# Two-layer attention and routing kernel: where a batch's statistics and its expert choice stand in the order of work

## The chip, the cores and the metric

The kernel runs on one core of one Trainium2 chip. The metric is the device time of one launch in microseconds. The core has five engines with a queue each: TensorE (PE, with its weight loads as PEld), VectorE (DVE), ScalarE (ACT), GpSimd (POOL) and SyncE (SP, which issues most of the transfers). Each queue is worked off in order, and the engines wait for one another with counting semaphores.

## What is computed

Input x is 4 batches of 1024 tokens of 128 numbers. Two layers follow, each of the form x = x + s · silu(f), where s is an attention and f a feed-forward network, both of the normalised xn = layernorm(x). Cut to what matters here:

```
xn = layernorm(x)
s  = attention(xn)            # 16 heads of 64, rope with cos/sin(position * rope_freqs), bias by distance
g  = silu(moe(xn))            # second layernorm with weights nw, nb; top-1 gate over 8 experts
x  = x + s * g
xn = layernorm(x)
# second layer: a recurrence over the tokens of each batch, per head (16 heads of 8)
q, k, v = xn @ q_w.T, xn @ k_w.T, xn @ v_w.T
lam = clip(sigmoid(decay) * (1 + 0.2 * sigmoid(tanh(xn @ cs_w1.T + b1) @ cs_w2.T + b2)), 0, 0.9995)
state_t = state_(t-1) * lam_t + k_t * v_t;   y_t = q_t . state_t;   s = y @ o_w.T
# its feed-forward network: one of 8 low-rank additions is chosen for each token
logits = xn @ gate_W.T + gate_b;   top1 = argmax(logits)
f  = relu(xn @ wi.T + wi_b + lora[top1](xn)) @ wo.T + wo_b
x  = x + s * silu(f)
```

## The kernel before

The program has three blocks one after the other: `before_heads` (the front: normalisation, routing, experts, q/k/v with rope), `attend` (the scores of 16 heads, by far the longest) and `layer1` (the second layer, here the last stage). A block starts when the block ahead of it has ended.

**Front.** Tokens lie on the partitions: a batch is 8 tiles of 128 tokens. SP issues the four batches of x first; ACT issues four small transfers of the rope frequencies. On VectorE `turns_of_angle` (L522 to L527, three instructions over 128x1024) multiplies positions by frequencies and finds the number of full turns; it waits for the frequencies. `stats(b)` (L494 to L508) waits for batch b of x, takes mean and variance (8 bn_stats, 8 bn_aggr) and five small instructions, and releases `var_ready`. GpSimd's `power(b)` then makes the reciprocal roots and the shift, ScalarE's `normalise(b)` the normalised rows, TensorE transposes them in the order of `turns` (xn0, xn1, a0, xn2, a1, xn3, a2, a3), ScalarE copies each out. `affine(b)` on VectorE makes the second norm. V rows are made between the transposes: TensorE, ScalarE (`v_high`), GpSimd (`v_low`), a transfer out. `reduced_angle` finishes the angles (they share tiles with nothing that the statistics use), the routing follows once all logits are there, and then 64 units of rope. The order on VectorE is written out: L537 `turns_of_angle()`, L538 `stats(0)`, then stats 1 and 2, affine 0, stats 3, affine 1 to 3, `reduced_angle`.

**Last stage.** It has N = 32 steps, 8 (FE) for each of 4 batches. Step n of the recurrence is: TensorE `made_rows(n)` (four matmuls for batch 0, L1710; two for the others, L1713), VectorE `scan(n)` (a product L1488 and a scan L1492), GpSimd's product with q (L1589), TensorE `share(n)` (16 matmuls, L1766), which stands two steps later in TensorE's queue. Two buffers are in rotation: made_rows(n) waits for scan(n-2), scan(n) for the product n-2.

Everything else is a list of jobs, `steps_of_layer1` (L1288), placed into the steps. In step n TensorE does made_rows(n), then the jobs of step n, then share(n-2). Each job writes the next of two PSUM banks in turn, so a job waits until the job two places before it has been taken out by ScalarE or VectorE. VectorE takes out the jobs of step n behind scan(n). The jobs:

- `turn`, `c1`, `c2`, `k`, `q`, `v`: transposes, decay, keys, queries and values of a batch. Those of batch 0 up to `c2` stand in `first`, ahead of step 0. TensorE's c1 waits itself for the transposes to be copied out; `z` does not.
- `z`: 16 matmuls, the logits and the low-rank products of a batch. ScalarE copies them out. `GATE_AT` names for each batch the step in which VectorE does `best_gate` (L1454: adds the bias, subtracts the maximum); ScalarE's Exp comes a step later, VectorE's `route` (L1461: first index of the maximum, one-hot, masked rows z_masked) two steps later.
- the network's feed, in eight halves j of 512 tokens: `zt` j (transposes z_masked, waits for `route`; VectorE takes out a part of it at L1503), `hid` j,0 to 3 (L1748 and L1749; the first waits for that part of zt), `out` j (32 matmuls, L1754). They are spread from step FFN_FROM to step 31 by a cost (zt 1, hid 2, out 7): `at[FFN_FROM + done * span // total].append(job)` with `span = FE * B - FFN_FROM`. After each second out ScalarE does the Silu of that batch (`SILU_AT`), and GpSimd the last product and sum of it.

Before the change the first steps hold (the number is the batch, or the half for zt, hid and out): step 0 both halves of q0 and of turn1; step 1 z0 z1 c1 v; step 2 c1 k v; step 3 k c2; step 4 c2 zt0 hid0,0 hid0,1; step 5 q hid0,2 hid0,3 zt1; step 6 q out0; step 7 hid1,0. In GATE_AT stand steps 1, 4, 12 and 20.

Between the loops VectorE has `stats(2)` in step 2 and `split_lora` (two small instructions) in step 1. ScalarE does norm(1) (8 instructions) ahead of its jobs of step 0.

Of the kernel before, what the change touches and what calls it, by code (L numbers as in the profile page):

```python
# [21 lines left out]
B, S, D = 4, 1024, 128  # L22
# [17 lines left out]
M_FIRST, W_SLOTS, E_SLOTS = 4, 10, 40  # L40
V_FIRST, V_MID = 18, 8
DMA = 16
FE, FFN_FROM = 8, 4
MAGIC = 12582912.0
TWO_PI_1 = 6.28125
TWO_PI_2 = 0.00193500518798828125
# [130 lines left out]
def before_heads(nc, K, io, sb, ps, sem):  # L177
# [116 lines left out]
    with nc.Block() as block:  # L294
# [196 lines left out]
        def _(v):  # L491
# [30 lines left out]
            def turns_of_angle():  # L522
                v.wait_ge(pos_made, 1)
                v.wait_ge(fr_in, 4 * DMA)
                ch.link(v.tensor_scalar(ang, pos, freq[:, 0:1], None, ALU.mult))
                ch.link(v.tensor_scalar(tn, ang, 1.0 / (2.0 * math.pi), MAGIC, ALU.mult, ALU.add))
                ch.link(v.tensor_scalar(tn, tn, MAGIC, None, ALU.subtract))  # L527

            def reduced_angle():
                for part in (TWO_PI_1, TWO_PI_2, TWO_PI_3):  # L530
# [3 lines left out]
                v.scalar_tensor_tensor(out=tn, in0=ang, scalar=-1.0, in1=ang, op0=ALU.mult,  # L534
                                       op1=ALU.max).then_inc(sin_arg, 1)

            turns_of_angle()  # L537
            stats(0)  # L538
            stats(1)
            stats(2)  # L540
            affine(0)
# [749 lines left out]
def steps_of_layer1():  # L1291

    at = [[] for _ in range(FE * B)]
    at[0] += [("q", 0, 0), ("q", 0, 1)]
    at[1] += [("z", 0, 0)]
    for b in range(1, B):
        n = FE * (b - 1)
        for f, jobs in enumerate(([("turn", b, 0), ("turn", b, 1)], [("z", b, 0), ("c1", b, 0)], [("c1", b, 1), ("k", b, 0)],
                                  [("k", b, 1), ("c2", b, 0)], [("c2", b, 1)], [("q", b, 0)], [("q", b, 1)])):
            at[n + f] += jobs  # L1300
    for b in range(1, B):
        for c in range(2):
            at[FE * (b - 1) + 1 + c].append(("v", b, c))
    feed = [("zt", 0, 0)] + [("hid", 0, i) for i in range(FT)]
    for j in range(NR):
        if j + 1 < NR:
            feed.append(("zt", j + 1, 0))
        feed.append(("out", j, 0))
        if j + 1 < NR:
            feed += [("hid", j + 1, i) for i in range(FT)]  # L1310
    cost = {"zt": 1, "hid": 2, "out": 7}
    total, done, span = sum(cost[job[0]] for job in feed), 0, FE * B - FFN_FROM
    for job in feed:
        at[FFN_FROM + done * span // total].append(job)
        done += cost[job[0]]
    return [("turn", 0, 0), ("turn", 0, 1), ("c1", 0, 0), ("c1", 0, 1), ("k", 0, 0), ("k", 0, 1), ("c2", 0, 0), ("c2", 0, 1)], at


def layer1(nc, K, io, sb, ps, sem):
# [7 lines left out]
    aux_made, by_act, by_dve, lam_raw = sem("aux_made"), sem("aux_by_act"), sem("aux_by_dve"), sem("lam_raw")  # L1327
# [39 lines left out]
    dve_takes = [job for job in jobs if job[0] in ("v", "zt", "out")]  # L1367
    act_nth = {job: k + 1 for k, job in enumerate(act_takes)}
    dve_nth = {job: k + 1 for k, job in enumerate(dve_takes)}
    GATE_AT = [1] + [FE * (b - 1) + 4 for b in range(1, B)]  # L1370
    SILU_AT = [step_of["out", 2 * b + 1, 0] + 1 for b in range(B)]

    def bank(job):
# [15 lines left out]
    with nc.Block() as block:  # L1389
# [48 lines left out]
        def _(v):  # L1438
# [72 lines left out]
            for n in range(N):  # L1511
# [3 lines left out]
                if n % FE == 2 and n // FE + 2 < B:  # L1515
                    stats(n // FE + 2)
                if n in GATE_AT:
                    best_gate(GATE_AT.index(n))
                if n - 2 in GATE_AT:
                    route(GATE_AT.index(n - 2))  # L1520
                if n == 1:
# [81 lines left out]
        def _(act):  # L1603
# [72 lines left out]
            for n in range(N):  # L1676
# [6 lines left out]
                if n % FE == 1 and n >= FE:  # L1683
                    take_share(n // FE - 1)
                if n - 1 in GATE_AT:
                    act.wait_ge(max_sub, GATE_AT.index(n - 1) + 1)
# [9 lines left out]
        @block.tensor  # L1696
        def _(pe):
            def made_rows(n):

                b, f = n // FE, n % FE  # L1700
                if n >= 2:
                    pe.wait_ge(scanned, n - 1)
                if n == FE:
                    pe.wait_ge(sel_made, 8)
                if n >= FE:
                    pe.wait_ge(vp_in[b % 2], vp_due(b))
                at = slice(64 * (f % 2), 64 * (f % 2) + 3 * H)
                for c in range(2):
                    if n < FE:
                        mm = pe.matmul(pj[n % 2][:, half(c)], wv[:, f, :], tokens(b, c),  # L1710
                                       start=True, stop=True)
                    else:
                        mm = pe.matmul(pj[n % 2][:, half(c)], SEL[at, :, :].rearrange("r h e -> r (h e)"),  # L1713
                                       VP[b % 2][at, f // 2, half(c)], start=True, stop=True)
                mm.then_inc(made, 1)

            def aux(job):
                kind, b, c = job
                a, dst = place[job], bank(job)
                if a >= 2:  # L1720
                    before = jobs[a - 2]
                    if before in dve_nth:
                        pe.wait_ge(by_dve, dve_nth[before])
                    else:
                        pe.wait_ge(by_act, act_nth[before])
                if kind == "turn":
                    pe.wait_ge(xn_ready, 2 * b + c + 1)
                    for k in range(4):
                        mm = pe.transpose(dst[:, k * P:k * P + P], XN[:, b % 2 * BT + 4 * c + k, :], K.ident[:])  # L1729
                elif kind == "c1":  # L1730
                    pe.wait_ge(by_act, act_nth["turn", b, c])
                    mm = pe.matmul(dst[0:D // 4, :], c1w[:], tokens(b, c), start=True, stop=True)  # L1732
                elif kind == "c2":
                    pe.wait_ge(by_act, act_nth["c1", b, c])
                    mm = pe.matmul(dst[:], c2w[:], C1[:, half(c)], start=True, stop=True)
                elif kind == "z":
                    for t in range(BT):
                        mm = pe.matmul(dst[:, t * NZ:t * NZ + NZ], XNT[:, (b * BT + t) * P:(b * BT + t + 1) * P], wz[:],  # L1738
                                       start=True, stop=True)
                elif kind == "v":  # L1740
                    mm = pe.matmul(dst[:], wvc[:].rearrange("p f h -> p (f h)"), tokens(b, c), start=True, stop=True)  # L1741
                elif kind == "zt":
                    pe.wait_ge(zm_ready, b // 2 + 1)
                    for t in range(4):
                        mm = pe.transpose(dst[0:3 * ER, t * P:t * P + P], ZM[:, 4 * (b % 4) + t, :], K.ident[:])
                elif kind == "hid":
                    pe.wait_ge(by_dve, dve_nth["zt", b, 0])
                    pe.matmul(dst[:], wi[:, c * P:c * P + P], XNT[:, half(b)], start=True, stop=False)  # L1748
                    mm = pe.matmul(dst[:], lb[:, c * P:c * P + P], ZT[:, half(b)], start=False, stop=True)  # L1749
                elif kind == "out":  # L1750
                    for i in range(FT):
                        pe.wait_ge(by_act, act_nth["hid", b, i])
                        for t in range(4):
                            mm = pe.matmul(dst[:, t * P:t * P + P], hT[b % 2][:, i, t * P:t * P + P], wo1[:, i, :],  # L1754
                                           start=(i == 0 and t == 0), stop=(i == FT - 1), skip_group_check=True)
                else:
                    mm = pe.matmul(dst[:], (wk if kind == "k" else wq)[:], tokens(b, c), start=True, stop=True)  # L1757
                mm.then_inc(aux_made, 1)

            def share(n):  # L1760
                b, f = n // FE, n % FE
                pe.wait_ge(weighed, n + 1)
                if f == 0 and b >= 1:
                    pe.wait_ge(s1_out, b)
                for t in range(BT):
                    mm = pe.matmul(so[:, t, :], WT[:, n % 2, t * P:t * P + P], wo[:, f, :],  # L1766
                                   start=(f == 0 and t % 4 == 0), stop=(f == FE - 1), skip_group_check=True)
                mm.then_inc(shared, 1)

            pe.wait_ge(w_in, 7 * DMA)  # L1770
            for job in first:
                aux(job)
            pe.wait_ge(vo_in, 2 * DMA)
            pe.wait_ge(wz_in, 2 * DMA)
            for n in range(N):
                made_rows(n)
                if n == 0:
                    pe.wait_ge(base_ready, 3)
                if n == FFN_FROM:
                    pe.wait_ge(lb_ready, 1)  # L1780
                for job in steps[n]:
                    aux(job)
                if n >= 2:
                    share(n - 2)
            share(N - 2)
            share(N - 1)
# [110 lines left out]
```

## Time and profile before

| | us |
|---|---|
| three runs | 1762.02, 1763.08, 1769.20 |
| median | 1763.08 |
| the profiled execution, its own time | 1762.21 |
| its span | 1760.5 |
| TensorE, VectorE, GpSimd, ScalarE busy | 1621.9, 1496.0, 1413.8, 1177.6 |

The profiled execution stands 1.7 us above its span and 0.9 us below the median. All times in the rows further down are microseconds from the start of the span. The page shows the span in slices: up to about 51 us is the front's normalisation, the rope units end at some 390 us, `attend` ends at 1515 us, the last stage takes the rest. A row of the timeline gives start, duration (of one instruction, or of a group that follows itself), engine, line, operation, tiles and shapes, and in brackets how long the engine was idle before it and what ended that.

### The profile page before, as it was taken

The numbers are of one execution on the slowest core, as the hardware profiler recorded it, in microseconds if no ns is written. First come the engines' busy times: TensorE is split into PE (matmuls) and PEld (weight loads), VectorE is DVE, ScalarE is ACT, GpSimd is POOL, SyncE is SP. The second block draws the span as 40 slices with busy tenths as digits, with TensorE's granted clock in tenths as the row PEclk, the third lists the DMA queues.
The fourth block names the chain that finished last, engine by engine and source line by source line (L and its number), as shares of the span: only waits on it lengthen the run. The fifth ranks groups of instructions, "written<-read, shape, count | busy, mean of one in ns | idle before, by whom it ended". The sixth has DMA issues, their size and how long they took to land. (4 is left out here: it accounts for less than half of the span.)

```text
span 1760.5 us, 39216 instructions
## 1 busy us (share of the span) xinstructions
PE 1621.9 (92%) x12064; PEld 890.5 (51%) x12064; DVE 1496.0 (85%) x3046; ACT 1177.6 (67%) x1806; POOL 1413.8 (80%) x820
## 2 busy tenths in 40 slices
PE   4879989858999999999999999999999999689998
PEld 3435655423555555555555555555555555346666
DVE  7778978996888989898898989888898989567876
ACT  6536544537877878777877877787787877644441
POOL 5676847857999999999999999999999999553554
PEclk9899999988999999999999999999999999889999
DMA  5466856768989889889889989989989988500110
GB/s 161 136 182 191 225 157 184 197 201 189 177 193 218 186 180 233 181 184 228 181 190 213 194 176 221 194 183 210 198 189 199 210 179 171 120 18 1 31 31 25
DMA packets 735171, 296.46 MB, mean 168 GB/s; under 512 B 630192, under 2 KB 697778, under 8 KB 735104
## 3 DMA queue, kind: packets, MB, share of 16 engines
q1 hardware_dynamic: 732304, 292.17, 73.9%
q0 software_dynamic: 2048, 3.15, 0.9%
q8 instruction: 24, 0.39, 0.1%
q10 hardware_dynamic: 768, 0.53, 0.1%
q14 instruction: 27, 0.22, 0.0%
HBM read 101.34 MB, written 58.85 MB: 91 GB/s over the span
## 5 line engine op out<-in xcount | busy, mean ns | idle before, releaser
L1271 POOL TENSOR_TENSOR probs_lo<-probs 128x1024 bf16<-128x1024 f32 x512 | 953.7, 1895 | 80.5 <-ACT probs L1235 79.9
L1235 ACT ACTIVATE probs<-scores,neg_max 128x1024 f32<-128x1024 f32 x512 | 588.2, 1149 | 220.1 <-DVE neg_max L1153 211.4
L1153 DVE CUSTOM_DVE_ANT_0 scores<-score_ps,bias_tab 128x1024 f32<-128x1024 f32 x512 | 620.3, 1220 | 76.9 <-issue 69.8
L1067 PE MATMUL score_ps<-x 128*128 128x512 bf16 x1024 | 308.5, 383 | 31.5 <-PEq L294 17.8
L1083 PEld LDWEIGHTS turn_ps<-ident_bf,probs 128*128 128x128 bf16 x4096 | 261.1, 98 | 146.0 <-issue 55.9
L1083 PE MATMUL turn_ps<-ident_bf,probs 128*128 128x128 bf16 x4096 | 313.9, 219 | 0.2
L1102 PE MATMUL pv_ps<-probs_t_hi,v_hi_lo 128*128 128x512 bf16 x1024 | 263.6, 380 | 0.3 <-DVE share L1185 0.3
L1242 ACT COPY probs_t_hi<-turn_ps 128x1024 bf16<-128x1024 bf16 x256 | 253.8, 991 | 0.0
L439 POOL TENSOR_TENSOR qk_parts<-rotated,qk_parts 128x1024 bf16<-128x1024 f32 x64 | 137.4, 2152 | 84.0 <-ACT qk_parts L872 83.6
L1168 DVE COPY probs_t_hi<-turn_ps 128x1024 bf16<-128x1024 bf16 x256 | 172.6, 674 | 0.8 <-PE turn_ps L1083 0.8
L1589 POOL TENSOR_TENSOR q_state<-state,q_t 128x1024 f32<-128x1024 f32 x32 | 76.0, 2375 | 107.2 <-PE s_ps L1766 71.3
L1075 PE MATMUL score_ps<-x 64*128 64x512 bf16 x1024 | 155.9, 383 | 0.0
L1102 PEld LDWEIGHTS pv_ps<-probs_t_hi,v_hi_lo 128*128 128x128 bf16 x1024 | 84.4, 98 | 115.0 <-issue 27.5
L1107 PE MATMUL pv_ps<-probs_t_lo,v_hi_lo 128*64 128x512 bf16 x1024 | 134.7, 385 | 0.0
L1067 PEld LDWEIGHTS score_ps<-x 128*128 128x128 bf16 x1024 | 74.9, 98 | 116.2 <-issue 45.5
L728 PE MATMUL turn_or_qk_ps<-xn_t,wqk 128*128 128x512 f32 x256 | 124.4, 611 | 7.5 <-DVE rotated L609 7.5
L1235 ACT ACTIVATION_READ_ACCUMULATOR probs<-scores,neg_max 128x1 f32 x512 | 96.2, 188 | 0.0
L1119 PE MATMUL pv_ps<-wo_parts,out_t_hi 128*128 (+1 forms) x512 | 90.9, 220 | 5.0 <-DVE out_t_lo L1176 2.3
L603 DVE TENSOR_TENSOR rope_cos<-turn_or_qk_ps,cos_table 128x1024 f32<-128x1024 f32 x64 | 78.0, 1219 | 17.5 <-PE turn_or_qk_ps L728 17.0
L609 DVE TENSOR_TENSOR rotated<-turn_or_qk_ps,rope_cos 128x1024 f32<-128x1024 f32 x64 | 78.4, 1225 | 15.3 <-POOL qk_parts L439 9.4
L1120 PE MATMUL pv_ps<-wo_parts,out_t_hi 128*128 (+1 forms) x512 | 89.3, 220 | 0.0
L1121 PE MATMUL pv_ps<-wo_parts,out_t_lo 128*128 (+1 forms) x512 | 89.1, 219 | 0.0
(236 smaller groups left out, 2311.1 us busy)
## 6 DMA issues: line engine op xcount, KB each, us to landing
x<-qk_parts SPq DMA_DIRECT2D x192, 256.0 KB, 3.4
qk_parts<-qk_parts SPq DMA_DIRECT2D x252, 128.0 KB, 2.5
v_hi_lo<-v_parts SPq DMA_DIRECT2D x64, 256.0 KB, 3.0
bias_tab<-bias_by_distance SPq DMA_DIRECT2D x64, 240.0 KB, 3.8
v_parts<-bias_tab SPq DMA_DIRECT2D x52, 256.0 KB, 2.9
probs_t_lo<-probs_lo SPq DMA_TRANSPOSE x512, 3.2
v_stacked<-v_three SPq DMA_DIRECT2D x72, 32.0 KB, 1.9
g<-in_x SPq DMA_DIRECT2D x4, 512.0 KB, 6.3
```

The source lines that it names most:

```text
L439: g.tensor_tensor(parts[n % QR][:, 2 - 2 * hi:4 - 2 * hi, :], rq[n % QR][:], parts[n % QR][:, 2 * hi:2 * hi + 2, :], ALU.subtract).then_in ...
L728: mm = pe.matmul(pp[n % 2][:, a * CH:a * CH + CH], K.wqk[:, g4, 2 * w + a, :], rows, start=True, stop=True)
L1067: pe.matmul(sp_[n % 2][:, cs], QB[s][:, q], KK[s][:, cs], start=True, stop=False)
L1075: mm = pe.matmul(sp_[i][:, cs], (QK, QB)[c][s][rows, q], (KK, QK)[c][s][rows, cs], start=False, stop=True)
L1083: mm = pe.transpose(tp[n % 2][:, k, :], PRB[n % NP][:, k * P:k * P + P], ident16[:])
L1102: mm = pe.matmul(ov[i][:], VV[h][:, k, :], PT[:, r:r + 4, k, :], start=(k == 0), stop=False, skip_group_check=True)
L1107: mm = pe.matmul(ov[c][c * DH:c * DH + DH], VV[h][:, k, 0:DH], LO[:, r:r + 4, k, :], start=False, stop=(k == BT - 1), skip_group_check=True)
L1153: v.tensor_tensor_reduce(SB[n % 2][:], sp_[n % 2][:], TB[s][:, j:j + S], -SCALE, 3.0e38, ALU.add, ALU.min, neg_max[:, n % 16:n % 16 + 1]). ...
L1168: v.tensor_copy(PT[:, n % U, :, :], tp[n % 2][:]).then_inc(hi_dve, 1)
L1235: act.activation(PR[n % NP][:], SB[n % 2][:], ACT.Exp, bias=neg_max[:, m:m + 1], scale=-1.0, accum_out=row_sum[:, m:m + 1]).then_inc(exped, 1)
L1242: act.copy(PT[:, n % U, :, :], tp[n % 2][:]).then_inc(hi_act, 1)
L1271: g.tensor_tensor(LQ[n % NL][:], PR[n % NP][:], PRB[n % NP], ALU.subtract).then_inc(low_made, 1)
```

## The change

It has four parts. In the front `stats(0)` stands ahead of `turns_of_angle()`. In the last stage the job z of batch 0 moves from step 1 to the head of step 0, with a wait of TensorE for the copy of that batch's second transposed half. `GATE_AT` for batch 0 moves from 1 to 0, and with it best_gate to step 0, Exp to step 1 and route to step 2. FFN_FROM goes from 4 to 5: the feed is spread over 27 steps instead of 28.

```diff
-FE, FFN_FROM = 8, 4
+FE, FFN_FROM = 8, 5
...
+            stats(0)
             turns_of_angle()
-            stats(0)
             stats(1)
             stats(2)
             affine(0)
...
     at = [[] for _ in range(FE * B)]
-    at[0] += [("q", 0, 0), ("q", 0, 1)]
-    at[1] += [("z", 0, 0)]
+    at[0] += [("z", 0, 0), ("q", 0, 0), ("q", 0, 1)]
...
-    GATE_AT = [1] + [FE * (b - 1) + 4 for b in range(1, B)]
+    GATE_AT = [0] + [FE * (b - 1) + 4 for b in range(1, B)]
...
                 elif kind == "z":
+                    pe.wait_ge(by_act, act_nth["turn", b, 1])
                     for t in range(BT):
```

After it the first steps hold: step 0 z0, both halves of q0 and of turn1; step 1 z1 c1 v; steps 2 and 3 as before; step 4 c2; step 5 q zt0 hid0,0 hid0,1; step 6 q hid0,2 hid0,3 zt1; step 7 out0. Of the later steps, 10 gets zt2 and out1 (they stood in 9), 17 gets zt4 and out3 (they stood in 16); from step 23 on only zt7 moves (from 26 to 27). Silu of the first batch goes from step 10 to 11, of the second from 17 to 18; the last two stay.

## Rows read from the trace of the kernel before

**Rows 1.** Busy time by engine in two stretches: from:to, length, busy (count), PEclk, DMA, GB/s.

```profile
70.00:400.00 330.00, 278.43 (x1021) 153.71 (x1022) 284.37 (x286) 153.20 (x222) 224.15 (x138) 0.95 0.68 188
...
1568.90:1747.00 178.10, 170.06 (x981) 115.92 (x981) 128.71 (x133) 71.20 (x109) 89.06 (x41) 0.99 0.09 22
```

**Rows 2.** Timeline of VectorE in the front.

```profile
7.54 0.75 DVE L525 TENSOR_SCALAR rotated<-rotated,freq 128x1024 f32<-128x1024 f32 x1 [7.54 <-DMA freq<-in_freqs]
...
9.79 1.65 DVE L498 BATCH_NORM_STATS2 ln_six<-g 128x6 f32<-128x128 f32 x8
...
12.94 1.64 DVE L498 BATCH_NORM_STATS2 ln_six<-g 128x6 f32<-128x128 f32 x8
...
19.65 2.19 DVE L517 SCALAR_TENSOR_TENSOR s<-g,ln_rstd,attn_nw_rows 128x128 f32<-128x128 f32 x8 [0.34 <-ACT g L810]
...
51.72 0.49 DVE L549 COPY logits<-step_ps 128x320 f32<-128x320 f32 x1 [4.52 <-PE step_ps L679]
```

**Rows 3.** Timeline of SP's queue: the four batches of x are issued.

```profile
0.82 3.81 SPq L308 DMA_DIRECT2D g<-in_x  x4
```

**Rows 4.** Issue to landing: the four transfers of x; the last of the frequencies.

```profile
DMA to landing us min/median/max: 4.0/6.3/7.9
...
freq<-in_freqs ACTq DMA_DIRECT2D x1, 0.1 KB, 5.2
```

**Rows 5.** Timeline of ScalarE in the front: the first two batches normalised.

```profile
16.34 6.33 ACT L810 ACTIVATE g<-g,ln_shift,ln_rstd 128x128 f32<-128x128 f32 x16 [12.35 <-POOL ln_shift L417]
```

**Rows 6.** Chain of work that ended last, early last stage: start, length, what.

```profile
1575.43 1.72 PE made_ps L1710 x4
1577.15 0.86 PE aux_ps L1757 x2
...
1580.61 1.79 PE s_ps L1766 x16
```

**Rows 7.** Timeline of TensorE, steps 0 to 4 of the last stage.

```profile
1537.16 1.14 PE L1729 MATMUL aux_ps<-ident,xn 128*128 128x128 f32 x8 [1.57 <-ACT q_t L1640]
...
1539.86 3.66 PE L1738 MATMUL aux_ps<-gate_lora_a,xn_t 128*128 128x40 f32 x32
...
1564.71 1.06 PE L1745 MATMUL aux_ps<-ident,z_masked 128*96 128x128 f32 x4 [4.39 <-DVE z_masked L1474]
1568.89 2.04 PE L1748 MATMUL aux_ps<-xn_t,wi 128*128 128x512 f32 x2 [3.12 <-DVE z_t_parts L1503]
```

**Rows 8.** Timeline of VectorE, steps 1 to 4, and step 6 for comparison.

```profile
1546.81 0.40 DVE L1457 TENSOR_TENSOR z_rows<-z_rows,gate_b 128x64 f32<-128x64 f32 x1
...
1547.65 0.41 DVE L1478 CAST lora_b_parts<-lora_b_f 96x512 bf16<-96x512 f32 x1
...
1548.81 1.23 DVE L1488 TENSOR_TENSOR made_ps<-made_ps,k_t 128x1024 f32<-128x1024 f32 x1
1550.07 2.29 DVE L1492 TENSOR_TENSOR_SCAN state<-lam,made_ps 128x1024 f32<-128x1024 f32 x1
...
1559.71 2.38 DVE L1466 TENSOR_TENSOR route<-route,iota 128x64 f32<-128x64 f32 x1
...
1589.40 0.23 DVE L1466 TENSOR_TENSOR route<-route,iota 128x64 f32<-128x64 f32 x1
```

**Rows 9.** Timeline of GpSimd: its product of step 3.

```profile
1559.67 2.34 POOL L1589 TENSOR_TENSOR q_state<-state,q_t 128x1024 f32<-128x1024 f32 x1 [3.77 <-DVE state L1492]
```

**Rows 10.** Timeline of ScalarE: norm(1), and the load ahead of Exp.

```profile
1533.46 3.18 ACT L1614 ACTIVATE xn<-x,ln_shift,ln_rstd 128x128 f32<-128x128 f32 x8
...
1553.61 1.28 ACT L1688 ACT_TABLE_LOAD   x1
```

**Rows 11.** Two stretches of 2 us in the last stage, columns as above.

```profile
1562.00:1564.00 2.00, 0.00 (x0) 0.00 (x0) 1.90 (x7) 0.00 (x0) 2.00 (x3) 0.86 0.00 0
1572.00:1574.00 2.00, 2.00 (x8) 1.19 (x7) 0.00 (x0) 0.55 (x2) 0.00 (x0) 0.58 0.25 52
```

**Rows 12.** TensorE's waits from 1570 to 1748: total us, times, longest.

```profile
PE aux_ps L1748 <- ACT lam L1636: 3.1, 3, 1.5
```

## The prediction

> **What bounds the kernel now.** I read the stretches first [rows 1]. In the front's 64 rope units (70 to 400 us) VectorE is busy 284 of 330 us, and in the last stage, from 1568.9 to 1747, TensorE 170 of 178. So the last stage is TensorE's from 1568.9 on; ahead of that the timelines show it waiting. Three places matter to the change.
>
> In the front VectorE's first instruction waits 7.54 us for the rope frequencies, and only behind the three angle instructions, at 9.79, does it begin on the first batch of x [rows 2]. That batch was issued at 0.82 and is the shortest of four landings, 4.0 us: it lay there from 4.8 [rows 3, 4]. ScalarE's normalising starts at 16.34, after 12.35 us of idleness put down to GpSimd's shift, the next link behind the statistics [rows 5]. VectorE then works through with 0.34 us of idleness before affine(0) at 19.65.
>
> In the last stage TensorE idles 4.39 us for the masked rows of route(0) and 3.12 us more for VectorE's part of zt0, which stands behind scan(4); hid0,0 starts at 1568.89 [rows 7]. VectorE is the bound of that stretch: its chain runs from scan(2) at 1548.81 without a gap through a v part, stats(2), scan(3), route(0), scan(4) and the zt part [rows 8].
>
> The clock: from 1562 to 1564 TensorE did nothing and its granted clock averaged 0.86, from 1572 to 1574 it was 0.58, though busy throughout [rows 11]. It had fallen from 2.4 to 1.2 GHz in the wait, and the first of hid0,0 took 2.04 us instead of about 1.
>
> **The change part by part.**
>
> *Statistics first.* Nothing is removed or added; stats(0) and the angles change places. stats(0) takes 12.94 - 9.79 = 3.15 us, the angles 9.79 - 7.54 = 2.25 [rows 2]. New order: stats(0) from about 4.95 to 8.1; the angles to 10.35 (the last frequencies, issued at some 2.2, take 5.2 and are there at 7.4 [rows 4], so they no longer hold anything up); stats(1) to 13.5 and stats(2) to 16.65. The last x, issued before 4.63, needs at most 7.9, so no batch is late. affine(0) wants the first normalised rows: GpSimd and ScalarE had them 16.34 - 9.79 = 6.55 us after stats(0) began plus half of the 6.33 us of two batches, now 4.95 + 6.55 + 3.2 = 14.7. So VectorE is the later, and affine(0) starts at 16.65 instead of 19.65: 3.0 earlier. Batch 1's statistics end at 13.5 instead of 9.79 + 2 x 3.15 = 16.1, only 2.6 earlier, but stats(3) and all that VectorE orders behind affine(0) comes 3.0 earlier. What then leads to the logits at 51.72 is a chain of transposes, copies, v parts and their transfers, each started by the one before. VectorE waits 4.52 us there for TensorE [rows 2], so the angles could end later, unseen. The logits come 3.0 earlier, less whatever the parts that move by 2.6 hold back. I take 2.95; the bounds are 1.5 (the clock, or a transfer of v that meets the early loads) and 3.2. Nothing behind it is tied to a fixed time, so rope units and scores pass it on.
>
> *Logits and routing a step sooner.* z0 costs half of 3.66 us for z0 and z1 = 1.8 [rows 7], now in step 0. Its new wait, for the copy of turn 0,1, is free: that copy is before step 0. But q0's second half now uses the bank that z0 leaves, and ScalarE copies z0 out only behind norm(1), 1533.46 + 3.18 = 1536.64 [rows 10], plus an estimated 0.45. The second q starts at about 1537.1, where the transposes started before, and these follow 1.1 later, as the two copies alternate. made_rows(1) is 1.1 late, step 1 is 1.8 shorter, so what follows in step 1 is 0.7 earlier. best_gate(0) leaves VectorE's step 1, where it takes 1547.65 - 1546.81 = 0.85 [rows 8], for the wait ahead of scan(1): free. Scan(2) starts 0.7 + 0.85 = 1.5 earlier, at 1547.3. Exp's table load of 1.28 [rows 10] now stands ahead of step 2's tanh, whose bank the second v part wants; I estimate 0.65 of VectorE's waiting from it (half of the load; the rest lies beside scan(2)). If tanh needs a load again, it is 1.28 more.
>
> route(0) stood against GpSimd's product: L1466 took 2.38 us and ended 0.1 after that product (1559.67 + 2.34 = 1562.01), where the same form takes 0.23 alone [rows 8, 9]. In step 2, behind stats(2), the product of that step is done by then, so I take 2.15 off; the bounds are 0 and 2.75.
>
> *The network a step later.* zt0's part on VectorE now stands behind scan(5), not scan(4). That is one more product and scan, 1550.07 - 1548.81 + 2.29 = 3.55 [rows 8], and best_gate(1) of step 4, about what best_gate(0) takes, 0.85; I take 0.75, since its first row already holds some waiting. hid0,0 starts at 1568.89 - 1.5 + 0.65 + 3.55 + 0.75 - 2.15 = 1570.2 (without the front's gain), **1.3 later** than now. But by then TensorE has done what it now does behind it: share(2) 1.79, made_rows(5) 1.72 and a q of 0.86 = 4.37 [rows 6]. Net 4.37 - 1.3 = **3.1 earlier**. The idleness moves: TensorE has no more work after zt0, about as long after made_rows(5) as now after made_rows(4), and I estimate one wait of 4 to 5 us, so its clock falls again, and the slow first two hid stay at their price.
>
> From there TensorE's work is the same in sum, in 27 steps instead of 28. It lost 178.10 - 170.06 = 8.0 us there [rows 1], the largest part 3.1 in three waits for the sigmoid copies [rows 12]. zt2 and out1 now share step 10 with a v part, zt4 and out3 step 17: each waits about 1 us for VectorE's part of v behind the scan. In return Silu leaves the steps of the c1 jobs. I take no change, with 2 us to either side. The tail from step 24 is as before.
>
> A rule is to be weighed here. That row of 2.38 beside 0.23, ending with the product, is a stall of a whole instruction. The Trainium skill, "SBUF — State Buffer", section "SBUF: two separate sides", says that a VectorE operation with two SBUF inputs and a GpSimd operation that reads SBUF exclude each other for a whole instruction. By that rule best_gate(0), right behind scan(0) when the product of step 0 starts, waits up to 2.3 us, and scan(1) begins at 1541.5 instead of 1541.2; the sum would be the same, since the v part behind it comes later anyway.
>
> **Sum:** 2.95 + 3.1 = 6.0; 1762.21 - 6.0 = 1756.2 for an execution like the profiled one, which is 0.9 under the median. I say **1756.5**.
>
> **The rivals.**
>
> *A, the clock holds.* If TensorE's wait for zt0 is short enough, hid0,0 and 0,1 run at 2.4 GHz and save about 2.4 more (the first alone 1.0 of 2.04 [rows 7]): 1753.8 or, with a better step pattern, 1752. Against it: I expect one wait of over 4 us, and 4.39 took the clock down. 0.13.
>
> *B, only the front gains.* The fuller steps 10 and 17 leave TensorE waiting 3 us more and eat the 3.1: 1759.3. For it: the bank order couples every job to VectorE's scan. Against: TensorE idles only 8.0 in 178 now. 0.19.
>
> *C, only the last stage gains.* The change doesn't do in the front what it says: the logits are bound by the v parts and their transfers, which wait for something other than VectorE. 1759.1. Against: ScalarE's first work waits on the statistics. 0.08.
>
> *D, slower.* Place: VectorE between scan(1) and zt0's part. best_gate(0), split_lora, stats(2) and route(0) all move against GpSimd's products, and each stalls a full 2.34 [rows 9]: 9.4 us. It decides from the point where hid0,0 starts 4.37 + 2.95 = 7.3 later than 1568.89. With all four it starts 1.3 + 9.4 = 10.7 later, the stage loses 9.4 - 3.1 = 6.3, the sum is 3.3 slower: 1765.5. Against: one such stall is seen there in five steps. 0.05.
>
> **Chances.** Forecast 0.55, own range 1754 to 1759; A 0.13, B 0.19, C 0.08, D 0.05. Low end: A with 2 us fewer waits, 1751.5. High end: B or C with the worse front and a run 0.9 above the profile, 1761.5. A measurement of this kernel can tell about 0.5% (8.8 us) from no change. Faster by more than that (under 1754.3) takes most of A and the forecast's lower edge: 0.17. Slower by more (over 1771.9) takes D with further loss: 0.03. Within: 0.80.
>
> **What would show it.** Right: bn_stats of the first batch at 4.9 to 5.0, angles from 8.1, affine(0) near 16.7, the logits' copy near 48.8; in the last stage (less the front's 3) best_gate(0) ahead of scan(1), TensorE's one wait of 4 to 5 us ahead of hid0,0, half clock behind it, made_rows(8) two to three us earlier than now. Wrong: the logits not 2.5 earlier; hid0,0 more than 4.4 later; TensorE's waits behind it well over 8 us; or a granted clock that stays full.

## The result, and the profile after

| | before | after |
|---|---|---|
| runs | 22 | 22 |
| median, us | 1767.27 | 1760.17 |
| lowest, us | 1762.02 | 1756.61 |
| the profiled execution, its own time | 1762.21 | 1762.45 |
| its span | 1760.5 | 1760.7 |

The ratio of the new kernel to the old one is 0.9968, with a 95% interval from 0.9956 to 0.998: 0.32% faster, less than the 0.5% that the prediction took as its bound. The interval lies below 1 all the same. The ratios are of fast runs alone: two slow ones of the kernel before, of 2690.35 us here and of 5571.03 beside runs 9 to 12 below, don't count in them. The means without them lie 5.6 us apart, the medians 7.1. The median of 1760.17 lies 1.2 above the range of 1754 to 1759 that the prediction gave. Yet the two profiled executions last the same, so a reader who had only these would find no gain. Why becomes clear from the trace, stretch by stretch.

**The front** did what the prediction says. Timeline of VectorE in the front, after (columns as in [rows 2]):

```profile
4.98 1.65 DVE L498 BATCH_NORM_STATS2 ln_six<-g 128x6 f32<-128x128 f32 x8 [4.98 <-DMA g<-in_x]
...
8.15 0.75 DVE L525 TENSOR_SCALAR rotated<-rotated,freq 128x1024 f32<-128x1024 f32 x1
...
16.70 2.19 DVE L517 SCALAR_TENSOR_TENSOR s<-g,ln_rstd,attn_nw_rows 128x128 f32<-128x128 f32 x8
...
48.67 0.49 DVE L549 COPY logits<-step_ps 128x320 f32<-128x320 f32 x1 [4.43 <-PE step_ps L679]
```

The first statistics start at 4.98 (forecast 4.95) and no longer wait for the frequencies, the angles stand at 8.15 (8.1), affine(0) at 16.70 (16.65), and the logits are copied at 48.67 (48.8) instead of 51.72 [rows 2]. The first rope unit starts at 63.09 instead of 66.07.

**In the rope units** the lead is lost. It is still 2.6 when VectorE has taken out the expert's output at 263.08 in the kernel before and at 260.49 after, and zero at the next unit, which starts at 266.73 and 266.75. TensorE's timeline there, before:

```profile
263.81 1.16 PE L752 MATMUL out_ps<-w,hidden_t 128*128 128x128 f32 x8 [2.76 <-DVE expert_out L630]
264.81 1.88 PE L728 MATMUL turn_or_qk_ps<-xn_t,wqk 128*128 128x512 f32 x4
```

and after:

```profile
261.23 2.07 PE L752 MATMUL out_ps<-w,hidden_t 128*128 128x128 f32 x8 [2.76 <-DVE expert_out L630]
263.09 3.62 PE L728 MATMUL turn_or_qk_ps<-xn_t,wqk 128*128 128x512 f32 x4
```

The wait ahead is the same, 2.76 us for the same instruction of VectorE. Behind it the same eight matmuls take 1.16 in one kernel and 2.07 in the other, and the four of the unit 1.88 and 3.62. The granted clock tells why. The stretch from 260 to 265 us, before and then after (columns as in [rows 1]: from:to, length, busy of PE, PEld, DVE, ACT and POOL, PEclk, DMA, GB/s):

```profile
260.00:265.00 5.00, 2.24 (x13) 1.41 (x13) 3.62 (x4) 1.62 (x2) 3.58 (x2) 1.00 0.68 184
```

```profile
260.00:265.00 5.00, 3.77 (x11) 2.74 (x12) 1.17 (x2) 0.13 (x1) 2.13 (x1) 0.56 0.91 227
```

It stayed at 2.4 GHz before and was at 1.2 GHz for most of the stretch after. Over all 64 units VectorE took 324.1 us from the first to the last instead of 320.4. Whether this belongs to the change is a question for the experiments.

**In the last stage** the wait ahead of the network is one, as foreseen, and the clock falls in it. TensorE's timeline after:

```profile
1564.83 1.02 PE L1757 MATMUL aux_ps<-xn_t,q_w 128*128 128x512 f32 x2
1565.69 0.60 PE L1745 MATMUL aux_ps<-ident,z_masked 128*96 128x128 f32 x4
1570.95 1.68 PE L1748 MATMUL aux_ps<-xn_t,wi 128*128 128x512 f32 x2 [4.66 <-DVE z_t_parts L1502]
1572.42 0.63 PE L1749 MATMUL aux_ps<-z_t_parts,lora_b_parts 96*128 96x512 bf16 x1
1572.85 1.91 PE L1748 MATMUL aux_ps<-xn_t,wi 128*128 128x512 f32 x2
```

One wait of 4.66 (forecast 4 to 5) stands in place of 4.39 and 3.12 [rows 7], and share(2), made_rows(5) and the q are done ahead of it. Further on the waits grew. All waits of TensorE from 1572 to 1747 (us in total, times, longest), before, all rows:

```profile
PE aux_ps L1748 <- ACT lam L1636: 3.1, 3, 1.5
PE aux_ps L1741 <- ACT cs_hidden L1625: 1.6, 1, 1.6
PE aux_ps L1745 <- DVE z_masked L1474: 1.2, 1, 1.2
PE aux_ps L1748 <- ACT k_t L1629: 0.5, 1, 0.5
PE aux_ps L1748 <- ACT xn_t L1623: 0.5, 2, 0.2
PE aux_ps L1745 <- DVE v_rest L1500: 0.4, 1, 0.4
PE aux_ps L1748 <- DVE v_rest L1500: 0.4, 1, 0.4
PE aux_ps L1754 <- ACT fhid L1652: 0.3, 1, 0.3
```

and after:

```profile
PE aux_ps L1748 <- ACT lam L1635: 3.6, 2, 2.3
PE aux_ps L1754 <- DVE v_rest L1499: 2.3, 2, 1.3
PE aux_ps L1754 <- ACT lam L1635: 1.1, 1, 1.1
PE aux_ps L1754 <- ACT fhid L1651: 0.7, 2, 0.3
PE aux_ps L1748 <- DVE v_rest L1499: 0.6, 1, 0.6
PE aux_ps L1748 <- ACT q_t L1639: 0.5, 1, 0.5
PE aux_ps L1748 <- ACT xn_t L1622: 0.2, 1, 0.2
```

That is 8.0 in sum before and 9.0 after; the waits for VectorE's v part (2.3, out1 and out3) and for one sigmoid copy of 2.3 are new. And the clock falls behind two of them. TensorE's timeline after, at steps where the kernel before ran at full clock:

```profile
1628.32 1.12 PE L1748 MATMUL aux_ps<-xn_t,wi 128*128 128x512 f32 x2 [2.34 <-ACT lam L1635]
...
1629.63 3.45 PE L1766 MATMUL s_ps<-o_w_rep,q_state 128*128 128x128 f32 x16
...
1686.99 5.47 PE L1754 MATMUL aux_ps<-wo_t,fhid 128*128 128x128 f32 x32 [1.05 <-ACT lam L1635]
```

A share takes 3.45 instead of 1.95, an out 5.47 instead of 3.84. Of the lead of some 4 us that the stage has at made_rows(8) (75.5 us behind its first load, 79.5 before), half a us is left at its end (244.6 and 245.2). So one profile against the other says: front 3.0 gained, rope units 3.7 lost, last stage 0.5 gained. The runs say 0.32%. The experiments had to tell what of this is the change and what is the draw of one execution.

### The profile page after: what moved, and what is told of

The parts are those of the page before. It is cut to its first block and busy times, and to the rows that moved or that the text cites. A ratio compares the mean times of both kernels' runs of the same rounds, so it can differ in the third digit from the quotient of the medians.

```text
span 1760.7 us, 39221 instructions
## 1 busy us (share of the span) xinstructions
PE 1627.8 (92%) x12064; PEld 893.6 (51%) x12064; DVE 1491.2 (85%) x3046; ACT 1179.4 (67%) x1807; POOL 1414.3 (80%) x820
## 5 line engine op out<-in xcount | busy, mean ns | idle before, releaser
L603 DVE TENSOR_TENSOR rope_cos<-turn_or_qk_ps,cos_table 128x1024 f32<-128x1024 f32 x64 | 78.0, 1219 | 21.1 <-PE turn_or_qk_ps L728 20.4
```

## The experiments

Two theories stood against each other. **Sum** (Theory 1 in what was expected of each run): both parts gain about what the prediction says, and the clock in the rope units is a draw that has nothing to do with the change. **Only the front** (Theory 2, rival B): the last stage gives its 3.1 back. A third, named in run 1, was that the rope units lose the front's gain for good. In each run I read the same marks: the length from the first to the last rope unit, and, from the last stage's first load (q_w), hid0,0, made_rows(31) and the end.

**1. The front alone.**

```diff
+            stats(0)
             turns_of_angle()
-            stats(0)
```

> The first part of the change alone: the first batch's statistics ahead of the angles. Theory 1 (the two parts add up, and what differs from run to run is the clock): the front's logits are copied at 48.7 as in the kernel after, against 51.7 before, unit 0 of rope starts 3.0 earlier, and where two executions lose the same time at half clock in the rope units the whole is 3 us shorter: ratio 0.9983, the last stage as before. Theory 2 (only the front gains): the same 3 us here, and it is all there is, ratio here equal to that of the whole change. Theory 3 (the front's gain is lost in the rope units for good): unit 0 is 3.0 earlier but unit 63 is not, in every execution, and the ratio is 1.000.

Measured: ratio 0.9991 (0.9979 to 1.0004), which by itself can't be told from no change. The logits at 48.45 and the first rope unit at 62.91 are those of the changed kernel. The units took 324.4 us, and the last stage, in which nothing was changed, 246.7 instead of 245.2. In this profile Theory 3 fits; runs 5 and 10 speak against it.

**2. The last stage alone.** All of the diff but the front.

> The second part alone: logits, best_gate and route of batch 0 a step sooner, the network from step 5; the front as before. Theory 1: ratio 0.9982 (3 us); from the last stage's first load hid0,0 starts 54.9 later (53.6 before), made_rows(8) 2 to 3 us sooner than before, and the stage ends sooner unless the clock falls in a wait. Theory 2: the stage's length from its first load to its last instruction is that of before within 0.5, because the fuller steps 10 and 17 wait 3 us more; ratio 1.000. Theory 3: 0.9968, the whole gain.

Measured: 0.9998 (0.9986 to 1.0009). The logits stay at 51.67. hid0,0 comes 55.3 behind the first load, the end 243.2. The rope units, of which no instruction is moved against another here, took 323.9 us. So the fall at unit 38 is not the front's doing.

**3. Logits and routing sooner, the feed as before.** FFN_FROM stays at 4; z0, GATE_AT and TensorE's wait as in the change.

```diff
-    at[0] += [("q", 0, 0), ("q", 0, 1)]
-    at[1] += [("z", 0, 0)]
+    at[0] += [("z", 0, 0), ("q", 0, 0), ("q", 0, 1)]
...
-    GATE_AT = [1] + [FE * (b - 1) + 4 for b in range(1, B)]
+    GATE_AT = [0] + [FE * (b - 1) + 4 for b in range(1, B)]
```

> Only logits, best_gate and route a step sooner; the network still from step 4, the front as before. Theory 1: VectorE's part of zt0 stands behind scan(4), hid0,0 starts 50.6 after the stage's first load instead of 53.6, TensorE waits about 5 us in one piece ahead of it and runs at half clock behind it; waits behind it as before, 8 us; the stage is 3.0 shorter, ratio 0.9983. If instead TensorE's waits behind hid0,0 grow, the stage gains under 1 us.

Measured: 0.9984 (0.9973 to 0.9995), the only one of the first four whose interval lies below 1. hid0,0 comes 50.7 behind the first load (expected 50.6), its wait for VectorE's part is 4.92. The stage takes 244.2 us, 1.0 less than in the profile of before, where 3.0 were expected. Of the lead at hid0,0 a part is lost again further on, though TensorE's waits there are 6.9 us and not more than before: the clock falls at a place where it held in the kernel before. TensorE's timeline of this run:

```profile
1622.36 2.03 PE L1748 MATMUL aux_ps<-xn_t,wi 128*128 128x512 f32 x2 [0.54 <-ACT k_t L1628]
...
1627.49 2.80 PE L1766 MATMUL s_ps<-o_w_rep,q_state 128*128 128x128 f32 x16
```

Behind the same wait of 0.54 us the kernel before took 1.12 for that first row, and 1.95 for the share.

**4. The feed a step later, the routing as before.** Only FFN_FROM from 4 to 5.

> Only FFN_FROM 5: logits and route where they were, the front as before. Theory 1: hid0,0 starts one scan and one best_gate later (4.3), 57.9 after the stage's first load, but TensorE has 4.37 of later work behind it by then: no change up to made_rows(8), and 0 to 2 us more of waits in steps 10 and 17: ratio 1.000 to 1.001. Theory 2 has the 3 us more of waits here: 1.0017. Best case for the later feed: the denser steps wait less and the ratio is below 0.999.

Measured: 1.0027 (1.0013 to 1.0041), slower. hid0,0 comes 61.1 behind the first load, 3.2 later than expected, behind one wait. TensorE's timeline of this run:

```profile
1568.00 0.60 PE L1745 MATMUL aux_ps<-ident,z_masked 128*96 128x128 f32 x4
1577.98 2.04 PE L1748 MATMUL aux_ps<-xn_t,wi 128*128 128x512 f32 x2 [9.38 <-DVE z_t_parts L1503]
```

Two things made up the 3.2, and VectorE's timeline shows both: 4.18 us of idleness ahead of its part of v, and a stall in best_gate(1):

```profile
1549.49 0.69 DVE L1500 TENSOR_TENSOR v_rest<-aux_ps,v_three 128x512 f32<-128x512 f32 x1 [4.18 <-ACT v_three L1646]
...
1571.56 2.09 DVE L1459 TENSOR_TENSOR z_rows<-z_rows,cols 128x64 f32<-128x64 f32 x1
```

The idleness was 2.59 in the kernel before. It is a clock fall again: TensorE waits 1.57 us for a q copy ahead of batch 1's first transposes [rows 7], and in this run the next matmuls of c1 took 1.92 instead of 1.04. In the profile of before the clock had held behind the same wait. So the later feed by itself costs time, and it gains only together with the sooner routing, if at all: the whole last stage (0.9998 in run 2) is not better than run 3 (0.9984).

**5. The whole again**, on another chip, with the next three beside it.

> The whole change once more, beside kernels that differ from it in one thing, on one chip. Theory 1 (two gains of 3 us that add up): ratio 0.9966, and in the profile unit 0 of rope at 63.1, hid0,0 54.9 after the last stage's first load. Theory 4 (what the parts alone measured, 1.1 and 0.3 us in the mean, is all): 0.999. Rope units: 320 to 325 us, as the clock falls there; the scores 1128.9 as in every profile so far.

Measured: 0.9972 (0.996 to 0.9984), median 1761.07. This is the same program as the one after the change, and its profile is 5.8 us shorter (span 1754.9): rope units 320.2 us, last stage 244.5. Its timeline at unit 38:

```profile
258.95 1.16 PE L752 MATMUL out_ps<-w,hidden_t 128*128 128x128 f32 x8 [2.76 <-DVE expert_out L630]
259.95 1.88 PE L728 MATMUL turn_or_qk_ps<-xn_t,wqk 128*128 128x512 f32 x4
```

The 2.76 are there to the hundredth, and the clock holds. So the 3.7 us lost in the rope units of the profile after are not a cost of the change: the same program ran without them, and runs 2 to 4, whose program up to the last stage is that of before, ran with them (323.9, 324.7 and 323.5 us). It is a draw of the execution or of the chip.

**6. VectorE's part of zt0 ahead of the scan.** The other way to shorten TensorE's wait: the front and the sooner routing, FFN_FROM 4, and in step 4 VectorE takes out zt0 before `scan(n)`.

```diff
+                for job in steps[n]:
+                    if job == ("zt", 0, 0):
+                        take(job)
                 scan(n)
...
-                    take(job)
+                    if job != ("zt", 0, 0):
+                        take(job)
```

> The whole change, but with the network from step 4, and VectorE takes its part of zt0 ahead of scan(4) instead of behind it. If that part is the wait ahead of hid0,0 (Theory 1), hid0,0 starts 47.2 after the stage's first load (54.9 in the whole change, 50.7 with the network from step 4), TensorE waits 1.4 instead of 4.7 us there, its clock holds at 2.4 GHz in the first two hid, and the stage is 239 us long instead of 243 to 245: ratio to before 0.995. If the stage is bound by VectorE's scans instead, it stays over 242.

Measured: 0.9947 (0.993 to 0.9963), median 1756.65. hid0,0 comes 49.6 behind the load instead of the expected 47.2, its wait is 2.33 instead of 1.4. Of the 2.4, 1.4 stand ahead: in this execution batch 1's transposes start 24.2 behind the load, 22.8 in the kernel after. Most of the rest is that VectorE stood ready but waited for ScalarE's copy of zt0, which I had left out:

```profile
1561.14 0.69 DVE L1502 TENSOR_TENSOR z_t_parts<-aux_ps,z_t_parts 32x512 bf16<-32x512 f32 x1 [0.89 <-ACT z_t_parts L1651]
```

The clock held: the first of the network took 1.10 and 1.02, TensorE's timeline of this run:

```profile
1561.98 1.10 PE L1752 MATMUL aux_ps<-xn_t,wi 128*128 128x512 f32 x2 [2.33 <-DVE z_t_parts L1502]
1562.91 0.38 PE L1753 MATMUL aux_ps<-z_t_parts,lora_b_parts 96*128 96x512 bf16 x1
1563.13 1.02 PE L1752 MATMUL aux_ps<-xn_t,wi 128*128 128x512 f32 x2
```

**7. In addition, the first product of each hid before the wait.** hid adds two products into one bank; only the second needs VectorE's part.

```diff
-                    pe.wait_ge(by_dve, dve_nth["zt", b, 0])
                     pe.matmul(...)   # wi
+                    pe.wait_ge(by_dve, dve_nth["zt", b, 0])
```

> As the one before, and the first matmul of each hid (with wi, which needs no zt) stands ahead of the wait for zt's part, so that only the second (lora) waits. hid0,0's wi matmul runs in the wait: 0.9 us more in the first half, nothing in the seven others, whose zt is long done. Stage 238 us, ratio to before 0.9945; no difference to the one before if TensorE does not bound the stage there.

Measured: 0.9934 (0.9917 to 0.9951), median 1754.88, against 1761.07 of the whole change on the same chip. The stage lasts 237.6 us instead of 244.5. TensorE's timeline:

```profile
1559.03 1.12 PE L1751 MATMUL aux_ps<-xn_t,wi 128*128 128x512 f32 x2 [1.05 <-ACT lam L1639]
1560.22 0.39 PE L1753 MATMUL aux_ps<-z_t_parts,lora_b_parts 96*128 96x512 bf16 x1
```

The wait of 4.66 has become one of 1.05, for a bank. This version beats both kernels.

**8. TensorE kept busy in the wait.** The changed kernel with five products more into hid0,0's own bank, ahead of the wait; the first real product starts the bank anew, so nothing of theirs is used (the trace counts each as two).

```diff
+                    if b == 0 and c == 0:
+                        for _ in range(5):
+                            pe.matmul(dst[:], wi[:, 0:P], XNT[:, half(b)], start=True, stop=True)
```

> The whole change with five matmul pairs more (wi, 4.3 us, into the bank that hid0,0 overwrites) in TensorE's wait for zt0's part; they compute nothing that is used. If the waiting takes the clock down and that is its only cost, hid0,0 starts at 54.9 as before or up to 0.3 later, hid0,0 takes 1.0 instead of 1.7 to 2.0 a pair, and the stage is 1 to 2.4 us shorter than that of the whole change. If the clock falls whatever TensorE does, nothing changes.

Measured: 0.9965 (0.995 to 0.9979), beside 0.9972 for the whole change. TensorE's timeline, and the stretch of 15 us around it:

```profile
1563.76 4.56 PE L1749 MATMUL aux_ps<-xn_t,wi 128*128 128x512 f32 x10 [0.24 <-ACT q_t L1639]
1568.15 1.05 PE L1751 MATMUL aux_ps<-xn_t,wi 128*128 128x512 f32 x2
```

```profile
1560.00:1575.00 15.00, 14.76 (x54) 7.76 (x53) 8.81 (x9) 6.29 (x13) 14.37 (x8) 1.00 0.17 37
```

The clock stays at 2.4 GHz and hid0,0 takes 1.05 instead of 1.82 in run 5. From hid0,0 to made_rows(8) it is 18.8 us, 20.6 in run 5. The stage is only 1.0 shorter (243.5 and 244.5), as hid0,0 itself came 0.7 later behind the load in this execution, and so did batch 1's transposes, far ahead of the added products. In the ratios the two can't be told apart.

**9 to 12. Before, front, last stage and whole, once more**, on a third chip, to see whether the parts add up and what profiles of the same program differ by.

> The kernel before, unchanged, for a second profile of it and as a measure of the comparison itself. Its ratio is 1.000 within 0.001. In its profile the scores take 1128.9. Theory 5 (the profile of before was a lucky draw of the clock): the rope units take about 324 us from unit 0 to unit 63 instead of 320.4, and the last stage 246 to 247 instead of 245.2. If instead the change had made the rope units slower, they are 320 to 321 here.

> The first part alone once more, beside the second alone and the whole on one chip. Additive parts (Theory 1): 2.5 to 3 us faster than before, ratio 0.9984. As measured the first time: 0.9991.

> The second part alone once more. Theory 1: 2 to 3 us, ratio 0.9985. As measured the first time: 0.9998. In the profile the last stage takes 243 to 244.7 from its first load.

> The whole change once more on the same chip. 5 to 5.7 us faster, ratio 0.997. If the parts add up, the ratios of the two runs before this one, less 1, sum to it within 0.0015; if the whole gains 3 us more than the sum, the parts help each other through the clock.

Measured: 1.0007 (0.9992 to 1.0021) for the kernel before against itself, 0.9983 (0.9968 to 0.9997) front, 0.9997 (0.9984 to 1.001) last stage, 0.9985 (0.9972 to 0.9998) whole. The rope units took 321.0, 320.5, 320.5 and 320.8 us: what run 9 was expected to show of them (324, the profile of before a lucky draw) did not come, and its last stage took 247.8, somewhat more than the 246 to 247 expected. The parts add up: 0.0017 and 0.0003 make 0.0020, and the whole has 0.0015, within the intervals. But the whole is 2.6 us here and not the 5 to 5.7 expected.

Nine profiles now have the last stage as it was or as changed (runs 3, 4 and 6 to 8 have it otherwise). Its parts, in us:

| | first load to hid0,0 | to made_rows(31) | to the end | sum |
|---|---|---|---|---|
| as before: before, runs 1, 9, 10 | 53.6, 55.1, 56.3, 55.0 | 175.4, 176.5, 175.8, 176.4 | 16.2, 15.1, 15.8, 15.3 | 245.2, 246.7, 247.8, 246.7 |
| mean | 55.0 | 176.0 | 15.6 | 246.6 |
| as changed: after, runs 2, 5, 11, 12 | 54.9, 55.3, 54.7, 55.6, 56.2 | 175.2, 173.3, 175.2, 175.7, 176.7 | 14.6 (all five) | 244.6, 243.2, 244.5, 245.9, 247.5 |
| mean | 55.3 | 175.2 | 14.6 | 245.1 |

So the last stage is 1.5 us shorter in the mean of the traces. Executions of one program lie up to 3 apart in it (244.6, 244.5 and 247.5 for the whole change), so the 1.5 has a standard error of about 0.9, and the small differences between the parts are means of few and scattered values. What follows from it is in the next section.

## Why the prediction was right, and where it was wrong

**The direction** held, and so did the statement that the gain stays under the 0.5% bound. The time did not: 1760.17 against 1756.5 and a range up to 1759. Two things failed, the base from which the sum was taken and the last stage's term in the sum. The sum was 6.0 of 1762.2 us, a ratio of 0.9966; the three measurements of the whole are 0.9968, 0.9972 and 0.9985, in the mean 0.9975 or 4.4 us, with about 1.2 to either side. The sum was too large by about a quarter, and it is the last stage's term that was.

**The base.** The prediction set its sum against the profiled execution, "which is 0.9 under the median". Three runs were too few: the median of 22 is 1767.27, and the profiled one was a short draw, 5.1 below it. From 1767.27 the sum of 6.0 gives 1761.3, 1.1 above the 1760.17 measured. Against this first measurement, where the kernels are 7.1 apart in the medians, the forecast of 1756.5 was 3.7 too low by the base, not by the sum.

**Statistics first** (2.95 taken). Every time of the step came out to within 0.15 us, and the first rope unit is 3.0 earlier. In time it gave 0.9991 and 0.9983, that is 1.6 and 3.0 us, both with more than 2 to either side. "Rope units and scores pass it on" is right: the scores take 1128.9 us in the kernel before and after alike, and at most 1130.8 in any profile. What the sentence left out is that the units by themselves draw 320 or 324 us. Summed over stretches of 4 us, the length times what the granted clock lacks of 1 is 11.6 to 12.1 in the profiles with 320 to 321 us, and 15 to 17 in those with 323.5 or more.

**Logits and routing sooner.** The second half of q0 waited 0.49 for z0's copy and the transposes 0.24 for the q copy, in place of one wait of 1.57. The tanh behind Exp needed no second table load and made TensorE wait 0.44; VectorE, for which 0.65 was taken, took its second v part at 1552.79 without a gap behind the scan. route(0) lost its stall, as taken, and its one-hot lost 0.6 besides (0.23 us instead of 0.82). Timeline of VectorE, after:

```profile
1539.27 0.20 DVE L1456 TENSOR_TENSOR z_rows<-z_rows,gate_b 128x64 f32<-128x64 f32 x1
...
1547.08 1.50 DVE L1477 CAST lora_b_parts<-lora_b_f 96x512 bf16<-96x512 f32 x1
...
1556.90 0.23 DVE L1465 TENSOR_TENSOR route<-route,iota 128x64 f32<-128x64 f32 x1
```

0.23 stands where 2.38 did [rows 8]. split_lora, though, grew from 0.41 to 1.50, and GpSimd's timeline says why:

```profile
1539.78 2.41 POOL L1588 TENSOR_TENSOR q_state<-state,q_t 128x1024 f32<-128x1024 f32 x1 [4.57 <-ACT q_t L1639]
...
1545.95 2.35 POOL L1588 TENSOR_TENSOR q_state<-state,q_t 128x1024 f32<-128x1024 f32 x1
```

The product of step 1 ends at 1548.30, the stalled instruction at 1548.58. In run 4 best_gate(1)'s 2.09 ended 0.08 after a product. So one of rival D's four stalls came, at half price, and scan(2) starts 33.3 behind the load instead of 33.5, only 0.2 earlier and not the 1.5 of the prediction. By the rule of the Trainium skill that the prediction weighed ("SBUF — State Buffer", section "SBUF: two separate sides") best_gate(0) would have waited too. It didn't, and that doesn't speak against the rule, by which the one that starts first goes through: the last of its three instructions starts at 1539.76, and the product, which waited for the q copy, only at 1539.78. I had put it right behind scan(0).

**The network a step later** (hid0,0 1.3 later, 3.1 net). In the first pair of profiles hid0,0 came 1.33 later behind the stage's first load, behind one wait of 4.66 and at half clock, as stated. That the 1.3 fits so well is luck: the 1.3 by which scan(2) came too late were met by the 0.65 taken for tanh, which wasn't paid, and the 0.6 of the one-hot. Over all profiles hid0,0 is only 0.35 later, because the old order pays something that one profile didn't show: its 1.57 wait ahead of the transposes took the clock down in runs 1, 4 and 9 and not in before's profile nor in run 10. The new order has no wait so long there, and no fall in any of its profiles: from the transposes to hid0,0 it takes 32.1 us in all five, the old order 31.7 and 31.6 without the fall and 33.1 and 34.4 with it (runs 1 and 9). What run 10 is later than the profile of before lies ahead of the transposes, which start 23.5 behind the load there and not 21.8.

The step that failed is **"I take no change, with 2 us to either side"** for all that comes behind hid0,0. If that held, the way from hid0,0 to made_rows(31) would be 1.3 + 3.1 = 4.4 shorter. It is 0.8 shorter. The 3.6 that are missing have two parts. TensorE's waits are 0.9 longer: 7.9 to 8.0 in the four profiles of the old order, 8.5 to 9.0 in the five of the new. In run 4, with nothing but FFN_FROM changed, they are 9.0; in runs 6 and 7, with FFN_FROM 4, they are 8.0. So this part is the later feed's. And the clock, summed as above, lacks 2.4, 3.4, 2.8 and 3.4 in the old order, 5.2, 3.4, 5.2, 5.6 and 7.8 in the new: 2.4 more in the mean, from falls behind the 2.34 and the 1.05 wait (in run 2 behind a wait of 1.27 alone); in the old order runs 1 and 10 have one such fall, behind a wait of 1.5. Together 3.3 of 3.6. I had counted the waits for v at 1 us each and nothing for what the clock does further on.

The price is that of rival B ("the fuller steps 10 and 17 leave TensorE waiting 3 us more"), its mechanism is shown for the 0.9 of waiting only. That the fuller steps also bring the falls is not shown, and run 3 speaks against it: there the feed is as before and the waits are 6.9, yet the clock lacks 7.4 from hid0,0 to made_rows(31), and the way is 178.9 instead of 176.0. Runs 6 and 7, also with the feed as before, lack 3.4 each, and run 4, with the later feed, 5.6. What decides where the clock falls in the last stage stays open.

**"The tail from step 24 is as before"** was wrong to the good side. Its instructions are the same, with the same wait of 1.99 ahead of the last share, but that share took 3.64, 2.66, 3.30 and 2.76 in the four profiles of the old order, and 2.05 in all others. TensorE's timeline before, and after:

```profile
1750.99 3.64 PE L1766 MATMUL s_ps<-o_w_rep,q_state 128*128 128x128 f32 x16 [1.99 <-POOL q_state L1589]
```

```profile
1752.81 2.05 PE L1766 MATMUL s_ps<-o_w_rep,q_state 128*128 128x128 f32 x16 [1.99 <-POOL q_state L1588]
```

That gives back 1.0. So the stage's 1.5 is made, in the means, of -0.35, +0.8 and +1.0. Run 3 has the old feed from step 4 on and is among those with 2.05; what sets the clock there stays open.

**The rivals.** A (the clock holds) did not come: it fell behind the wait ahead of hid0,0 (4.65 to 4.68) in all five profiles. Run 8 shows its price: 18.8 us from hid0,0 to made_rows(8), against 20.3 to 21.1 in the five, so 1.5 to 2.3, near the 2.4 taken. B came in its outcome, and for 0.9 of its 3 in its mechanism. C is out: the logits are copied at 48.5 to 49.0 in every profile with the new front, and at 51.3 to 52.6 in the others. D needs four full stalls and had half of one.

**What stays open.** By the ratios the last stage alone is worth 0.4 and 0.5 us (0.9998, 0.9997, each with 2 to either side), by the traces 1.5, by the whole less the front 2. These agree within their intervals, and no run here narrows it. Nor do they tell why the clock fell behind the 2.76 wait in the profile of after and in all four of the first chip (runs 1 to 4), and held in that of before and in all eight of the second and third: that the chip has a part in it is possible, and wasn't tried, as no program was profiled twice on one chip.

## What to carry to other kernels

Ask of a later start not only what it costs where it stands, but which full steps it makes: moving a spread-out feed by one step laid two jobs beside a v part in two steps, and TensorE's waits grew by 0.9 us. And an order of work is not priced by its waits alone: half clock behind waits of 0.5 to 2.3 us cost more here than the waits that were added. A wait is better shortened by what it waits for (run 6 moved one small instruction ahead of a scan, run 7 put the independent half of a product ahead of the wait: 0.9934 together) than by filling it with work from further on. And one profile is one draw: set the sum against a median of many runs, and compare stretches in several profiles before a loss is put down to the change.

## What the runs showed of the hardware

The same wait can take TensorE's clock down in one execution and leave it in the next: 2.76 us at unit 38 (0.56 and 1.00), 1.57 us ahead of the transposes. A fall came behind a wait of 1.05 us, 7 us behind one of 1.27, and did not come in run 6 behind 2.33 nor in run 2 behind 2.34. In run 3 the clock was down behind a wait of 0.54, behind which it held in the kernel before. The Trainium skill, "TensorE: Matmul & The Clock Gate", section "What's actually happening", says that the window in which TensorE's activity is judged is free-running and does not start anew with the kernel. The traces agree with it, as the same program met both outcomes at the same instruction, but none of them shows that window.

How much this moves the time could be read from the 22 runs of the changed kernel: their granted clock over the whole span lies between 0.973 and 0.982, and the span falls by 1.25 us for each 0.001 of it, with a scatter of 1.15 us around that line. So most of the spread of 12 us between runs of this program goes with the clock. In the 35 runs of the kernel before beside run 1 the slope is about the same, 1.22, with a scatter of 1.4.
